# Feed-forward weights rounded by GpSimd, attention's last bias loaded as a column, all orders written anew

## Chip, cores and metric

One core of one Trainium2 chip runs the kernel. The metric is the device time of one execution in microseconds (us). The engines are TensorE (PE; its weight loads are listed apart as PEld), VectorE (DVE), ScalarE (ACT), GpSimd (POOL) and SyncE (SP).

## What is computed

The input is x, 16 sequences of 256 tokens with 128 features. Two blocks follow each other, each as x + layernorm(block(layernorm(x))).

```
n  = ln(x, g, b)
W1 = gelu(n @ h1_w1 + h1_b1) @ h1_w2 + h1_b2        # 128 -> 512 -> 128
W2 = gelu(n @ h2_w1 + h2_b1) @ h2_w2 + h2_b2
t  = tril(W1 @ W2^T) @ n
t  = ln(gelu(t), g, b);  x1 = x + t
out = x + gelu(ln(x1, g, b) @ fm_w1 + fm_b1) @ fm_w2 + fm_b2      # attention block

h = silu(x @ w1 * s1) * (x @ w2 * s2)               # feed-forward block, 128 -> 512
h = gelu(h @ h1 * hs1);  h = gelu(h @ h2 * hs2)     # 512 -> 512, twice
out = h @ w3 * s3                                   # 512 -> 128
```

## The kernel before

**Tiling.** The 4096 tokens are cut into 8 chunks of 512 (N = 512, four tiles of 128 tokens). Activations inside the blocks lie transposed, features on partitions and 512 tokens along the free axis. The last chunk's feed-forward part is cut into two halves of 256 tokens, numbered 7 and 8.

**Precision.** Each product is made of values split into a rounded high half and a low half, both fp32r. An output tile takes three matmuls per block of weights: low weights by high input, high by high, high by low. The feed-forward weights are ternary, so their low halves are expected to be zero. The kernel tests that: `lo_block` (L339) subtracts on GpSimd, `lo_sum` (L472) adds up the absolute values on ScalarE, `lo_test`, `lo_count` and `lo_raise` (L738 to L743) make a flag, and TensorE reads it and branches into `stream` (L1191) with or without the third matmul. With zero low halves the feed-forward products take two.

**Weights.** SyncE loads six pieces of the attention weights into `raw`, with parts of x between them, then six pieces of the feed-forward weights into the same buffer (five of 1024 columns, one of 512; `F_PIECES`, L117). `attn_w_hi` (L457) rounds an attention piece on ScalarE and `attn_w_lo` (L717) subtracts on VectorE. `ffn_w_hi` (L467) rounds a feed-forward piece on ScalarE, with one copy. A feed-forward piece 0 to 2 is loaded when two attention pieces are used up, pieces 3 to 5 when `lo_sum` of pieces 0 to 2 is done.

**Engines.** ScalarE does gelu and every eviction of a high half twice over: `up_hi` (L504) writes the rounded gelu, `up_act` (L512) writes the whole gelu back to the PSUM bank, and VectorE's `up_lo` subtracts the one from the other (all such subtractions run through `low`, L715). The feed-forward layers do the same with `layer_hi`, `layer_act` and `layer_lo`. VectorE also has the statistics and the layernorms; of these `n_first` (L761) and `n_second` (L772) read two SBUF operands, as `attn_w_lo` does. GpSimd has small layernorm steps (`x_s_` L326, `rstd` L345), `n_low` (L335), two steps on x (`xr_scale`, `xr_b`), and the x output.

**Bias of the last layer.** `fm_b2` is the attention's last bias as a column, read by `fm_evict` (L542). SyncE loads it as a row of 512 bytes into a corner of `M`. `fm_bias_product` (L1083) on TensorE turns it into a column with one matmul against a one, next to the four matmuls that make `fm_bias`, and `fm_bias_add` (L726) copies it out of the bank on VectorE.

**Order.** Nothing is scheduled at run time. Each engine has one list of calls, written out by hand or by a planner, that interleaves the chunks; semaphores (`Steps`) hold the engines together. `TURNS` (L43) gives for each of the eight PSUM banks the order in which groups of results use it, and `bank_free` (L1036) waits for the group before. So an engine that waits holds up everything behind it in its list.

```
            def ffn_w_hi(i):                                  # ScalarE, L467
                c0, c1, at = F_PIECES[i]
                act.wait_ge(ffn_in[i], 16)
                nc.scalar.activation(Fw[0][:, c0:c1], raw[:, at:at + c1 - c0], ACT.Copy).then_inc(*ffn_hi.done(0, i))
            def lo_block(n):                                  # GpSimd, L339
                i, c0, at = F_BLOCKS[n]
                pool.wait_ge(*ffn_hi.at(0, i))
                nc.gpsimd.tensor_tensor(Fw[1][:, c0:c0 + DI], raw[:, at:at + DI], Fw[0][:, c0:c0 + DI].bitcast(f32),
                                        ALU.subtract).then_inc(*ffn_lo.done(0, n))
```

## Time and profile before

| what | value |
|---|---|
| median of 3 runs | 365.7 us (365.67 to 366.59) |
| span of the profiled execution, first to last instruction | 362.6 us |
| mean granted TensorE clock | 0.996 |
| busy: PE / DVE / ACT / POOL | 97% / 88% / 84% / 41% of the span |
| instructions: PE / DVE / ACT / POOL | 1788 / 954 / 552 / 213 |
| HBM traffic | 6.57 MB read, 2.10 MB written, 24 GB/s over the span |

The times listed are those of the three runs; the profiled execution has its span alone in the page, 3.1 us under the median. What lies around the span (start and end of the program) is not in it. Busy time counts an engine as busy from the start to the end of an instruction. Matmuls are pipelined and their ends are modelled, so that a busy TensorE need not be one at its peak; the same holds to a lesser degree for the other engines, whose instructions start before the end of the one ahead. In a timeline or a list of waits, "<-" and a name behind an idle time say what ended it. The rows leave out the numbers of a buffer, so fm_b2 stands there as fm_b.

### The profile page before, as it was taken

To read this page: it belongs to the slowest core of one execution; us is meant where nothing else is said; L and a number is where in the kernel's file an instruction comes from. 1 tells how busy PE (TensorE), PEld (TensorE's weight loads), DVE (VectorE), ACT (ScalarE), POOL (GpSimd) and SP (SyncE) were. 2 spreads that over 40 slices of the span, in tenths; PEclk is the share of its full clock that TensorE was granted. 3 is DMA by queue.
4 is the path that set the end of the run, shared out by engine and by line. 5 is a ranking of instruction groups with operands and counts; after the bars stand their busy time and mean duration, and the time that the engine had idled before them with its cause. 6 is when DMAs were issued, how large, how long until landed. Compare 5 with 4: busy or idle time off the path is not lost.

```text
span 362.6 us, 6039 instructions
## 1 busy us (share of the span) xinstructions
PE 350.1 (97%) x1788; PEld 289.2 (80%) x1788; DVE 319.9 (88%) x954; ACT 305.2 (84%) x552; POOL 147.2 (41%) x213
## 2 busy tenths in 40 slices
PE   6989999999999999999999999999999999999993
PEld 5867687778888888888888888888888887788992
DVE  5889999999999999889989989998969998886936
ACT  5999999997779979988599888897799569959892
POOL 4168842860546052504750286003920174044411
PEclk9999999999999999999999999999999999999998
DMA  7507020000000000000010001000000001001111
GB/s 233 174 14 245 4 60 1 1 2 1 3 0 0 2 0 2 17 13 2 1 29 3 0 0 33 0 1 2 1 0 2 0 2 31 0 2 29 32 30 33
DMA packets 8804, 9.08 MB, mean 25 GB/s; under 512 B 577, under 2 KB 6722, under 8 KB 8770
## 3 DMA queue, kind: packets, MB, share of 16 engines
q1 hardware_dynamic: 8226, 8.41, 7.7%
q8 instruction: 16, 0.26, 0.3%
q10 hardware_dynamic: 544, 0.26, 0.2%
q14 instruction: 18, 0.15, 0.1%
HBM read 6.57 MB, written 2.10 MB: 24 GB/s over the span
## 4 chain that ended last, share of the span: by engine, by line
PE 67%; ACT 13%; DVE 10%; issue 5%; DMA 2%; POOL 1%; SPq 1%; POOLq 0%; DVEq 0%; ACTq 0%
PE bank L1224 8%; PE bank L1226 8%; PE bank L1240 6%; PE bank L1241 6%; PE bank L1123 4%; PE bank L1104 4%; PE bank L1108 4%; PE bank L1105 4%; PE bank L1120 4%; PE bank L1121 4%; PE bank L1206 4%; PE bank L1209 4%; ACT h_hidden_hi L510 3%; PE bank L1046 2%; ACT bank L515 2%
## 5 line engine op out<-in xcount | busy, mean ns | idle before, releaser
L715 DVE TENSOR_TENSOR ffn_gate_lo<-bank,ffn_gate_hi 128x512 fp32r<-128x512 f32 (+1 forms) x72 | 44.1, 626 | 6.0 <-ACT bank L584 4.9
L510 ACT ACTIVATE h_hidden_hi<-bank,cols 128x512 fp32r<-128x512 f32 x64 | 46.1, 760 | 3.5 <-PE bank L1108 3.2
L515 ACT ACTIVATE bank<-bank,cols 128x512 f32<-128x512 f32 x64 | 45.1, 739 | 0.3
L715 DVE TENSOR_TENSOR h_hidden_lo<-bank,h_hidden_hi 128x512 fp32r<-128x512 f32 x64 | 43.0, 681 | 2.5 <-ACT bank L515 2.5
L584 ACT ACTIVATE bank<-bank,cols 128x512 f32<-128x512 f32 (+1 forms) x72 | 43.7, 620 | 0.7
L1224 PE MATMUL bank<-ffn_gate_hi,ffn_w_hi 128*128 128x512 f32 (+1 forms) x108 | 40.5, 381 | 0.2 <-DVE ffn_gate_lo L715 0.2
L1226 PE MATMUL bank<-ffn_gate_lo,ffn_w_hi 128*128 128x512 f32 (+1 forms) x108 | 39.3, 370 | 0.2 <-DVE ffn_gate_lo L715 0.2
L578 ACT ACTIVATE ffn_h_hi<-bank,cols 128x512 fp32r<-128x512 f32 (+1 forms) x36 | 23.0, 646 | 13.5 <-PE bank L1226 8.3
L578 ACT ACTIVATE ffn_gate_hi<-bank,cols 128x512 fp32r<-128x512 f32 (+1 forms) x36 | 23.2, 647 | 10.6 <-PE bank L1226 8.3
L364 POOL TENSOR_TENSOR XR<-X,ln_x_r 128x512 f32<-128x512 f32 x8 | 8.3, 1042 | 53.6 <-DVE bank L861 53.4
L715 DVE TENSOR_TENSOR ffn_h_lo<-bank,ffn_h_hi 128x512 fp32r<-128x512 f32 (+1 forms) x36 | 22.0, 626 | 8.0 <-ACT bank L584 7.8
L1206 PE MATMUL bank<-yT_hi,ffn_w_hi 128*128 128x512 f32 (+1 forms) x72 | 26.9, 378 | 0.0
L1123 PE MATMUL bank<-h_hidden_lo,attn_w_hi 128*128 128x512 f32 x64 | 25.8, 402 | 1.1 <-DVE h_hidden_lo L715 1.0
L569 ACT ACTIVATE ffn_gate_hi<-bank 128x512 fp32r<-128x512 f32 (+1 forms) x36 | 19.8, 560 | 8.0 <-DVE bank L906 8.0
L1240 PE MATMUL bank<-ffn_h_hi,ffn_w_hi 128*128 128x512 f32 (+1 forms) x72 | 26.4, 375 | 0.0
L1104 PE MATMUL bank<-aT_hi,attn_w_lo 128*128 128x512 f32 x64 | 25.9, 405 | 0.5 <-DVE attn_w_lo L715 0.5
L1209 PE MATMUL bank<-yT_lo,ffn_w_hi 128*128 128x512 f32 (+1 forms) x72 | 26.2, 369 | 0.0
L1120 PE MATMUL bank<-h_hidden_hi,attn_w_lo 128*128 128x512 f32 x64 | 26.0, 406 | 0.0
L1224 PE MATMUL bank<-ffn_h_hi,ffn_w_hi 128*128 128x512 f32 (+1 forms) x72 | 26.0, 368 | 0.0
L1226 PE MATMUL bank<-ffn_h_lo,ffn_w_hi 128*128 128x512 f32 (+1 forms) x72 | 25.9, 367 | 0.0
L1241 PE MATMUL bank<-ffn_h_lo,ffn_w_hi 128*128 128x512 f32 (+1 forms) x72 | 25.8, 367 | 0.0
L1240 PE MATMUL bank<-ffn_gate_hi,ffn_w_hi 128*128 128x512 f32 (+1 forms) x72 | 25.8, 366 | 0.0
(164 smaller groups left out, 1132.3 us busy)
## 6 DMA issues: line engine op xcount, KB each, us to landing
raw<-ffn_w SPq DMA_DIRECT2D x5, 512.0 KB, 3.9
out<-X SPq DMA_DIRECT2D x7, 256.0 KB, 2.3
raw<-attn_w SPq DMA_DIRECT2D x6, 256.0 KB, 4.9
X<-x SPq DMA_DIRECT2D x3, 256.0 KB, 5.6
raw<-ffn_w SPq DMA_DIRECT2D x1, 256.0 KB, 3.2
X<-x ACTq DMA_DIRECT2D x1, 128.0 KB, 2.5
X<-x SPq DMA_DIRECT2D x1, 128.0 KB, 2.3
out<-X SPq DMA_DIRECT2D x1, 128.0 KB, 1.8
```

What stands on the lines that cost most here:

```text
L510: nc.scalar.activation(dst, bank(f"{L}u{j}", c)[:, :], ACT.Gelu, bias=bias_of(L, j)).then_inc(*hi[L].done(c, j))
L515: nc.scalar.activation(u[:, :], u[:, :], ACT.Gelu, bias=bias_of(L, j)).then_inc(*act2[L].done(c, j))
L578: nc.scalar.activation(dst, bank(f"{L}{j}", c)[:, span(c)], ACT.Gelu, scale=cols[:, C_HS[L] + j:C_HS[L] + j + 1]).then_inc(*hi[L].done(c, j))
L584: nc.scalar.activation(u, u, ACT.Gelu, scale=cols[:, C_HS[L] + j:C_HS[L] + j + 1]).then_inc(*act2[L].done(c, j))
L715: return nc.vector.tensor_tensor(dst, whole, high.bitcast(f32), ALU.subtract)
L1120: nc.tensor.matmul(bank(g, c)[:, :], Aw[1][:, w], buf[0][:, slot, :], start=(k == 0), stop=False)
L1206: nc.tensor.matmul(dst, Fw[0][:, w], yT[0][:, span(c)], start=not lo_pass, stop=False)
L1209: nc.tensor.matmul(dst, Fw[0][:, w], yT[1][:, span(c)], start=False, stop=True)\
L1224: nc.tensor.matmul(dst, Fw[0][:, w], high, start=(k == 0 and not lo_pass), stop=False)
L1226: last = nc.tensor.matmul(dst, Fw[0][:, w], low_, start=False, stop=(k == J - 1))
L1240: nc.tensor.matmul(dst, Fw[0][:, w], src[0][:, k, span(c)], start=(k == 0 and not lo_pass), stop=False)
L1241: last = nc.tensor.matmul(dst, Fw[0][:, w], src[1][:, k, span(c)], start=False, stop=(k == J - 1))
```

## The change

Six instructions move from ScalarE to GpSimd: `ffn_w_hi` becomes a `tensor_copy` on GpSimd, in that engine's list, and ScalarE's copies go. The bias row's load on SyncE, its matmul on TensorE and its copy on VectorE go; ScalarE's queue issues a load of `fm_b2` as a column of 128 times four bytes right at the start, and `fm_evict(0)` waits for it. All five lists and the eight strings of `TURNS` are written anew. Except for what is named above, each engine's list holds the same calls as before in another order. Of the lists and of `TURNS` the diff below keeps the first lines and those at which the order matters for the prediction.

```diff
--- before.py
+++ after.py
@@ -41,29 +41,28 @@
-    "rb.0 fb.0 h1d.1 h1u3.2 fmd.0 h2u0.3 h2u2.3 flag.0 fmd.1 q3.0 a2.0 b0.0 mT.2 fmu2.2 p3.1 fT.0 h1u1.5 fmu2.3 q1.2 "
-    "h1d.5 p0.3 s1.5 t.5 p0.4 p1.4 fmu1.5 s1.6 a1.4 b0.4 b3.4 p1.5 p3.5 a2.5 b3.5 fmu2.7 a0.6 yT.7 b3.6 q1.8 a2.7 "
-    "a3.8 b2.8",
...
+    "rb.0 h1u0.0 h1d.0 h1u1.1 h2u3.1 h2u1.2 fmu2.0 nT.3 oT.0 h2u3.3 q0.0 h1u0.4 a2.0 h1u3.4 yT.1 w3.0 fmu3.2 h2d.4 "
+    "b2.1 b3.1 q2.2 q3.2 a2.2 b3.2 p2.3 t.5 yT.4 w3.3 q1.4 s1.6 t.6 fmu2.6 fmu0.7 fmd.7 oT.7 b0.6 q0.8 a0.8 b1.7 b2.8 "
+    "fT.7",
...
@@ -136,7 +135,6 @@
         NF, XR, XRB = sb("NF", [P, T, D]), sb("XR", [P, T, D]), sb("XRB", [P, T, D])
         n_tok = halves("n_tok", [P, T, D])
         M, TG = sb("M", [P, T, D]), sb("TG", [P, N])
-        b2_row = M[0:1, 0, :]
         OTA = sb("OTA", [P, N])
         aT, mT, yT = halves("aT", [P, N]), halves("mT", [P, N]), halves("yT", [P, N])
         WT = {L: halves(f"{L}T", [P, N]) for L in ("h1", "h2")}
@@ -286,7 +284,6 @@
             attn_piece(0)
             attn_piece(1)
             attn_piece(2)
-            sp.dma_start(b2_row, rows[2:3, :]).then_inc(b2_in, 16)
             x_piece(1, 1, 2)
             for i in (3, 4, 5):
                 attn_piece(i)
@@ -336,6 +333,11 @@
                 pool.wait_ge(*n_hi.at(c))
                 nc.gpsimd.tensor_tensor(n_tok[1][:, :, :], NF[:, :, :], n_tok[0][:, :, :].bitcast(f32), ALU.subtract).then_inc(*n_lo.done(c))
 
+            def ffn_w_hi(i):
+                c0, c1, at = F_PIECES[i]
+                pool.wait_ge(ffn_in[i], 16)
+                nc.gpsimd.tensor_copy(Fw[0][:, c0:c1], raw[:, at:at + c1 - c0]).then_inc(*ffn_hi.done(0, i))
+
             def lo_block(n):
                 i, c0, at = F_BLOCKS[n]
                 pool.wait_ge(*ffn_hi.at(0, i))
@@ -429,24 +431,26 @@
-            x_s_(0); n_low(0); x_s_(1); x_s_(2); lo_block(0); lo_block(1); x_r(0); xr_scale(0); lo_block(2); xr_b(0)
-            lo_block(3); n_low(1); t_r(0); x_r(1); lo_block(4); lo_block(5); x1_r(0); lo_block(6); lo_block(7); x_s_(3)
-            lo_block(8); n_low(2); t_r(1); xr_scale(1); xr_b(1); lo_block(9); o_r(0); x_r(2); x1_r(1); lo_block(10); y_r(0)
-            y_centre(0); y_scale(0); o_shift_(0); n_low(3); x_s_(4); xr_scale(2); xr_b(2); o_r(1); t_r(2); x_r(3); x1_r(2)
...
+            x_s_(0); n_low(0); x_r(0); x_s_(1); ffn_w_hi(0); lo_block(0); ffn_w_hi(1); lo_block(1); lo_block(2); x_s_(2)
+            lo_block(3); ffn_w_hi(2); lo_block(4); n_low(1); xr_scale(0); t_r(0); lo_block(5); xr_b(0); ffn_w_hi(3)
+            x1_r(0); lo_block(6); ffn_w_hi(4); lo_block(7); x_r(1); ffn_w_hi(5); n_low(2); x_s_(3); lo_block(8)
+            lo_block(9); t_r(1); xr_scale(1); xr_b(1); x_r(2); o_r(0); x1_r(1); lo_block(10); o_shift_(0); y_centre(0)
+            y_r(0); y_scale(0); n_low(3); x_s_(4); xr_scale(2); o_r(1); xr_b(2); o_shift_(1); t_r(2); x1_r(2); y_centre(1)
...
             act.dma_start(X[:, 2:4, :], xv[:, 2:4, :]).then_inc(x_in_half, 16)
+            act.dma_start(fm_b2[:, :], rows[2:3, :].rearrange("o d -> d o")).then_inc(b2_in, 16)
             act.wait_ge(*consts.at(0, 0))
             nc.scalar.activation(warm[:, :], ones[:, :], ACT.Gelu)
...
-            def ffn_w_hi(i):
-                c0, c1, at = F_PIECES[i]
-                act.wait_ge(ffn_in[i], 16)
-                nc.scalar.activation(Fw[0][:, c0:c1], raw[:, at:at + c1 - c0], ACT.Copy).then_inc(*ffn_hi.done(0, i))
 
@@ -542,6 +541,8 @@
             def fm_evict(c):
                 if c:
                     act.wait_ge(*oT.at(c - 1))
+                else:
+                    act.wait_ge(b2_in, 16)
                 act.wait_ge(*down["fm"].at(c, J - 1))
                 nc.scalar.activation(OTA[:, :], bank("fmd", c)[:, :], ACT.Identity, bias=fm_b2[:, :]).then_inc(*fm_out.done(c))
 
...
-            rows_out(); attn_w_hi(0); attn_w_hi(1); n_high(0); nT_high(0); attn_w_hi(2); attn_w_hi(3); attn_w_hi(4)
-            up_hi("h1", 0, 0); up_hi("h1", 1, 0); up_act("h1", 0, 0); up_act("h1", 1, 0); up_hi("h1", 2, 0); up_hi("h2", 0, 0)
-            up_hi("h1", 3, 0); up_act("h1", 2, 0); up_act("h2", 0, 0); up_act("h1", 3, 0); up_hi("h2", 1, 0); up_hi("h2", 2, 0)
-            up_act("h2", 1, 0); up_hi("h2", 3, 0); nT_high(1); up_act("h2", 2, 0); up_act("h2", 3, 0); ffn_w_hi(0)
-            attn_w_hi(5); down_hi("h1", 0); down_hi("h2", 0); up_hi("h1", 0, 1); up_hi("h2", 0, 1); ffn_w_hi(1)
-            up_act("h2", 0, 1); score_hi(0, 0); up_hi("h1", 1, 1); score_hi(1, 0); up_hi("h1", 2, 1); up_act("h1", 0, 1)
...
-            layer_act("b", 2, 8); layer_hi("b", 3, 8); w3_evict(7); layer_act("b", 3, 8); w3_evict(8); last_store()
+            rows_out(); attn_w_hi(0); attn_w_hi(1); attn_w_hi(2); nT_high(0); attn_w_hi(3); n_high(0); up_hi("h1", 0, 0)
+            up_act("h1", 0, 0); up_hi("h1", 1, 0); up_hi("h1", 2, 0); up_act("h1", 1, 0); up_hi("h1", 3, 0)
+            up_hi("h2", 0, 0); up_act("h1", 2, 0); up_act("h2", 0, 0); up_hi("h2", 1, 0); up_act("h1", 3, 0)
+            up_hi("h2", 2, 0); up_act("h2", 1, 0); up_act("h2", 2, 0); nT_high(1); up_hi("h2", 3, 0); attn_w_hi(4)
+            up_act("h2", 3, 0); down_hi("h1", 0); attn_w_hi(5); up_hi("h1", 0, 1); down_hi("h2", 0); up_hi("h2", 0, 1)
+            up_act("h1", 0, 1); up_act("h2", 0, 1); up_hi("h1", 1, 1); score_hi(0, 0); up_act("h1", 1, 1); score_hi(1, 0)
...
+            layer_act("b", 3, 8); w3_evict(7); w3_evict(8); last_store()
@@ -725,7 +729,6 @@
 
             def fm_bias_add():
                 dve.wait_ge(*fm_b.at(0))
-                nc.vector.tensor_scalar(fm_b2[:, :], bank("fb", 0)[:, J:J + 1], 1.0, None, ALU.mult)
                 nc.vector.tensor_tensor(fm_bias[:, :], bank("fb", 0)[:, 0:J], cols[:, C_B1["fm"]:C_B1["fm"] + J], ALU.add).then_inc(*fm_b_added.done(0))
 
             def gate_constants():
...
-            x_st(0); x_ag(0); n_first(0); n_second(0); attn_w_lo(0); attn_w_lo(1); nT_low(0); x_st(1); x_ag(1); n_first(1)
-            attn_w_lo(2); attn_w_lo(3); up_lo("h1", 0, 0); up_lo("h1", 1, 0); n_second(1); up_lo("h1", 2, 0); up_lo("h2", 0, 0)
-            x_st(2); up_lo("h1", 3, 0); x_ag(2); up_lo("h2", 1, 0); nT_low(1); up_lo("h2", 2, 0); up_lo("h2", 3, 0)
-            attn_w_lo(4); down_lo("h1", 0); down_lo("h2", 0); attn_w_lo(5); fm_bias_add(); score_mask(0, 0); score_mask(1, 0)
...
-            layer_lo("b", 1, 8); layer_lo("b", 2, 8); layer_lo("b", 3, 8); last_stats(0); last_aggregate(0); last_centre(0)
-            last_stats(1); last_aggregate(1); last_centre(1); last_sum(0); last_sum(1)
+            x_st(0); x_ag(0); n_first(0); n_second(0); attn_w_lo(0); nT_low(0); x_st(1); attn_w_lo(1); attn_w_lo(2)
+            attn_w_lo(3); up_lo("h1", 0, 0); x_ag(1); n_first(1); fm_bias_add(); up_lo("h1", 1, 0); x_st(2)
+            up_lo("h1", 2, 0); n_second(1); up_lo("h2", 0, 0); up_lo("h1", 3, 0); up_lo("h2", 1, 0); x_ag(2); nT_low(1)
+            up_lo("h2", 2, 0); x_st(3); up_lo("h2", 3, 0); down_lo("h1", 0); attn_w_lo(4); down_lo("h2", 0); attn_w_lo(5)
...
+            m_norm(2); t_ag(3); x_ag(5); up_lo("h1", 3, 4); layer_lo("b", 0, 0); layer_lo("b", 1, 0); mT_low(2)
...
+            layer_lo("b", 3, 8); last_stats(0); last_aggregate(0); last_stats(1); last_centre(0); last_aggregate(1)
+            last_centre(1); last_sum(0); last_sum(1)
@@ -1086,9 +1093,7 @@
                 pe.wait_ge(cols_in, 16)
                 for j in range(J):
                     w = ATTN["fmu"] + j * P
-                    nc.tensor.matmul(bank("fb", 0)[:, j:j + 1], raw[:, w:w + P], cols[:, C_B:C_B + 1], start=True, stop=True)
-                pe.wait_ge(b2_in, 16)
-                last = nc.tensor.matmul(bank("fb", 0)[:, J:J + 1], b2_row, ones[0:1, :], start=True, stop=True)
+                    last = nc.tensor.matmul(bank("fb", 0)[:, j:j + 1], raw[:, w:w + P], cols[:, C_B:C_B + 1], start=True, stop=True)
                 last.then_inc(*fm_b.done(0))
 
             def up_mm(L, j, c):
...
-            up_mm("h1", 1, 0); up_mm("h2", 0, 0); up_mm("h2", 1, 0); up_mm("h1", 2, 0); up_mm("h1", 3, 0); fm_bias_product()
-            down_mm("h1", 0, 0); up_mm("h2", 2, 0); down_mm("h1", 1, 0); up_mm("h2", 3, 0); down_mm("h1", 2, 0); n_transpose(1)
...
-            scores(1, 2); m_transpose(1); down_mm("h1", 3, 3); up_mm("h2", 3, 3); down_mm("h2", 1, 3); up_mm("fm", 0, 1)
-            up_mm("fm", 1, 1); lo_count(); t_product(2); y_transpose(0); down_mm("h2", 2, 3); up_mm("fm", 2, 1)
+            up_mm("h1", 1, 0); up_mm("h1", 2, 0); up_mm("h1", 3, 0); up_mm("h2", 0, 0); fm_bias_product()
+            down_mm("h1", 0, 0); up_mm("h2", 1, 0); up_mm("h2", 2, 0); down_mm("h1", 1, 0); down_mm("h1", 2, 0)
...
+            down_mm("h2", 0, 3); down_mm("h2", 1, 3); up_mm("fm", 0, 1); up_mm("fm", 1, 1); t_product(2); lo_count()
+            up_mm("fm", 2, 1); y_transpose(0); down_mm("h2", 2, 3); down_mm("h2", 3, 3)
...
```

Up to `yT_low(0)`, the VectorE step behind the first feed-forward input, the new VectorE list holds the same calls as the old one but for `x_ag(5)`, which comes later now. Up to `yT_high(0)` the new ScalarE list holds the same calls but for the six copies. Up to `y_transpose(0)` the new TensorE list holds one call more, `up_mm("fm", 2, 1)`. Behind `y_transpose(7)` TensorE's remaining calls, and behind `yT_high(7)` ScalarE's, are the same as before, in another order.

## Rows read from the trace of the kernel before

**Rows 1.** The page, busy us of each engine (share of the span) x instructions
```profile
PE 350.1 (97%) x1788; PEld 289.2 (80%) x1788; DVE 319.9 (88%) x954; ACT 305.2 (84%) x552; POOL 147.2 (41%) x213
```

**Rows 2.** The page, chain of work that ended last, by engine
```profile
PE 67%; ACT 13%; DVE 10%; issue 5%; DMA 2%; POOL 1%; SPq 1%; POOLq 0%; DVEq 0%; ACTq 0%
```

**Rows 3.** By stretch: length; busy PE, PEld, DVE, ACT, POOL (x count); clock; DMA share, GB/s
```profile
10.00:30.00 20.00, 18.75 (x98) 15.10 (x97) 17.45 (x45) 19.98 (x35) 10.07 (x11) 1.00 0.36 115
30.00:80.00 50.00, 48.48 (x243) 37.84 (x242) 48.30 (x166) 49.74 (x88) 30.13 (x36) 1.00 0.13 39
80.00:300.00 220.00, 220.00 (x1089) 182.76 (x1088) 202.56 (x594) 181.73 (x317) 83.72 (x123) 1.00 0.02 5
300.00:350.00 50.00, 49.11 (x282) 41.70 (x281) 38.39 (x104) 42.79 (x91) 17.44 (x28) 1.00 0.06 18
```
**Rows 4.** Chain in order of time: start us, us on the chain, what
```profile
20.98 0.98 ACT ffn_w_hi L470
24.78 0.95 ACT ffn_w_hi L470
37.37 0.52 ACT ffn_w_hi L470
40.75 0.97 ACT ffn_w_hi L470
```

**Rows 5.** All waits of ScalarE, 10 to 80 us: total, times, longest
```profile
ACT attn_w_hi L465 <- DMA raw<-attn_w: 1.0, 1, 1.0
```

**Rows 6.** Longest wait of VectorE, 10 to 80 us: total, times, longest
```profile
DVE sc_lo L715 <- ACT sc_hi L528: 0.8, 2, 0.4
```

**Rows 7.** Timeline, first 12 us: start us, us, engine, line, operation
```profile
3.19 0.33 SPq L289 DMA_DIRECT2D M<-rows  x1
...
7.23 0.63 ACT L483 ACTIVATE n_tok_hi<-NF 128x512 fp32r<-128x512 f32 x1 [0.61 <-DVE NF L776]
...
9.88 0.63 ACT L465 ACTIVATE attn_w_hi<-raw 128x512 fp32r<-128x512 f32 x1 [1.02 <-DMA raw<-attn_w]
...
11.17 1.25 ACT L510 ACTIVATE h_hidden_hi<-bank,cols 128x512 fp32r<-128x512 f32 x2
```

**Rows 8.** Timeline of GpSimd: a fill, an operation with a broadcast operand, and one with two operands
```profile
1.02 0.32 POOL L318 MEMSET mask<- 128x256 f32 x1
...
26.69 1.04 POOL L364 TENSOR_TENSOR XR<-X,ln_x_r 128x512 f32<-128x512 f32 x1
27.69 1.29 POOL L342 TENSOR_TENSOR ffn_w_lo<-raw,ffn_w_hi 128x512 fp32r<-128x512 f32 x1
```

**Rows 9.** Timeline of VectorE, operations with two SBUF operands
```profile
11.73 1.29 DVE L715 TENSOR_TENSOR attn_w_lo<-raw,attn_w_hi 128x512 fp32r<-128x512 f32 x2
...
24.41 0.94 DVE L715 TENSOR_TENSOR attn_w_lo<-raw,attn_w_hi 128x512 fp32r<-128x512 f32 x1
...
32.83 1.14 DVE L769 SCALAR_TENSOR_TENSOR NF<-X,ln_x_mv,bc 128x128 f32<-128x128 f32 x4 [0.22 <-issue]
```

**Rows 10.** Timeline of GpSimd, what ran beside them
```profile
22.03 2.77 POOL L342 TENSOR_TENSOR ffn_w_lo<-raw,ffn_w_hi 128x512 fp32r<-128x512 f32 x2 [1.82 <-ACT ffn_w_hi L470]
...
31.44 1.30 POOL L337 TENSOR_TENSOR n_tok_lo<-NF,n_tok_hi 128x512 fp32r<-128x512 f32 x1
```

**Rows 11.** Timeline of VectorE, two small steps
```profile
25.27 0.14 DVE L728 TENSOR_SCALAR fm_b<-bank 128x1 f32<-128x1 f32 x1
25.34 0.14 DVE L729 TENSOR_TENSOR fm_bias<-bank,cols 128x4 f32<-128x4 f32 x1
...
79.05 0.36 DVE L705 BATCH_NORM_AGGREGATE ln_x_mv<-ln_x_st 128x2 f32<-128x6 f32 x4
```

**Rows 12.** Timeline of GpSimd, two of its long waits
```profile
52.62 1.30 POOL L337 TENSOR_TENSOR n_tok_lo<-NF,n_tok_hi 128x512 fp32r<-128x512 f32 x1 [2.95 <-ACT n_tok_hi L483]
...
61.94 1.04 POOL L364 TENSOR_TENSOR XR<-X,ln_x_r 128x512 f32<-128x512 f32 x1 [3.43 <-DVE bank L861]
```

**Rows 13.** Readers of the bias column: duration min/median/max ns, first and last start us
```profile
L546 ACT ACTIVATE OTA<-bank,fm_b x8: 680/688/722, 59.4 to 315.1; 128x512 f32<-128x512 f32 x8
```

**Rows 14.** Timeline, last 8 us
```profile
354.82 0.48 ACT L590 ACTIVATE raw<-bank,cols 128x256 f32<-128x256 f32 x1
355.20 0.44 ACT L584 ACTIVATE bank<-bank,cols 128x256 f32<-128x256 f32 x1
...
356.89 0.60 DVE L939 TENSOR_SCALAR raw<-bank,ln_f_mv 128x128 f32<-128x128 f32 x2
```

More of the change, by code:

```diff
@@ L445, in _ @@
+            x_end(6); x_shift(); last_rstd(0); last_rstd(1)
         @block.scalar
@@ new lines, in _ @@
+            layer_hi("b", 2, 2); layer_act("b", 2, 2); layer_hi("b", 3, 2); gate_tanh(0, 3); gate_tanh(1, 3)
+            up_hi("fm", 0, 4); layer_act("b", 3, 2); up_hi("fm", 1, 4); up_act("fm", 0, 4); up_act("fm", 1, 4)
+            up_hi("fm", 2, 4); score_hi(0, 5); w3_evict(2); up_act("fm", 2, 4); gate_tanh(2, 3); gate_hi(0, 3)
+            up_hi("h1", 0, 6); gate_hi(1, 3); up_hi("fm", 3, 4); up_act("fm", 3, 4); gate_tanh(3, 3); fm_evict(4)
+            score_hi(1, 5); gate_hi(2, 3); up_hi("h1", 1, 6); up_act("h1", 0, 6); gate_hi(3, 3); t_act(5)
@@ new lines, in _ @@
+            layer_act("b", 2, 3); down_hi("h1", 6); mT_high(5); yT_high(4); up_hi("h2", 3, 6); layer_hi("b", 3, 3)
+            layer_act("b", 3, 3); up_act("h2", 3, 6); gate_tanh(0, 4); up_hi("fm", 0, 5); up_act("fm", 0, 5)
+            up_hi("fm", 1, 5); gate_tanh(1, 4); up_hi("fm", 2, 5); up_act("fm", 1, 5); w3_evict(3); gate_hi(0, 4)
+            gate_tanh(2, 4); nT_high(7); down_hi("h2", 6); gate_hi(1, 4); up_act("fm", 2, 5); up_hi("fm", 3, 5)
+            up_act("fm", 3, 5); up_hi("h1", 0, 7); gate_hi(2, 4); gate_tanh(3, 4); up_act("h1", 0, 7); fm_evict(5)
@@ new lines, in _ @@
+            layer_act("b", 1, 5); yT_high(6); layer_hi("b", 2, 5); layer_act("b", 2, 5); layer_hi("b", 3, 5); mT_high(7)
+            gate_tanh(0, 6); gate_tanh(1, 6); layer_act("b", 3, 5); up_hi("fm", 0, 7); up_hi("fm", 1, 7)
+            up_act("fm", 0, 7); up_act("fm", 1, 7); gate_tanh(2, 6); up_hi("fm", 2, 7); gate_hi(0, 6); up_act("fm", 2, 7)
+            gate_hi(1, 6); up_hi("fm", 3, 7); up_act("fm", 3, 7); gate_tanh(3, 6); gate_hi(2, 6); fm_evict(7)
+            gate_hi(3, 6); w3_evict(5); layer_hi("a", 0, 6); layer_act("a", 0, 6); layer_hi("a", 1, 6)
```

512 lines of the change are left out of this document (255 added, 257 removed), and 39 rows, old and new, of the table TURNS.

## Prediction

> **What bounds the kernel now.** I read the busy table first. TensorE is busy for 350.1 of 362.6 us [rows 1], and 67% of the chain that ended last is TensorE's [rows 2]. That leaves 12.5 us of open idle time, but busy time flatters an engine whose matmuls overlap, so the next view is the stretches [rows 3]. From 80 to 300 us TensorE shows no idle time at all and its weight loads are busy for 182.76 of 220 us, 0.831 per us. From 10 to 80 us they are busy for 15.10 + 37.84 = 52.94 us, 0.756 per us. At the later pace those loads would have taken 52.94 / 0.831 = 63.7 us, so about 6.3 us of that stretch is TensorE running thin, of which only 70 − 18.75 − 48.48 = 2.8 us is shown as idle. From 300 to 350 us the loads keep 0.834, and 0.9 us is idle.
>
> Who holds it back before 80 us? ScalarE is busy for 19.98 of 20 and 49.74 of 50 us [rows 3], and its only wait there is one of 1.0 us for a load [rows 5]. VectorE is busy for 17.45 of 20 and 48.30 of 50 us: 2.55 us idle up to 30 us, 1.70 us after. GpSimd has 10 of 20 and 20 of 50 us free. The chain in order of time runs over ScalarE's copies of the feed-forward weights [rows 4]. So before 80 us ScalarE is the bound, VectorE stands 4.25 us behind it, and behind 80 us only TensorE counts. A time saved before 80 us is kept only if TensorE reaches its full stretch earlier; nothing saved on ScalarE after that is worth anything. The granted clock is 1.00 in all four stretches, the 2.4 GHz level, and is no term.
>
> **ScalarE's six copies.** On the chain a copy of 1024 columns takes 0.98, 0.95 and 0.97 us, that of 512 columns 0.52 [rows 4]. Five long and one short make 5 x 0.97 + 0.52 = 5.4 us taken from an engine without idle time: two copies (1.9 us) before 30 us, four (3.4 us) between 30 and 80. VectorE is next: with the same calls up to yT_low(0) it can win no more than its idle time. Before 30 us the bound is 1.9 us (ScalarE) against 2.55 (VectorE's idle), and I take 1.5. After 30 us it is 3.4 against 1.70, and I take half of the 1.70, 0.85: the idle time is made of short waits for a result just ordered (the longest kind 0.8 us in two waits, [rows 6]), and part of such a wait stays when ScalarE is faster. Sum −2.35 us, between 0 and −3.6.
>
> **VectorE's removed and moved steps.** The copy of the bias column goes: the next step starts 25.34 − 25.27 = 0.07 us later [rows 11]. x_ag(5), 0.36 us [rows 11], moves behind yT_low(0), into a stretch where VectorE has 17 us free of 220. Together −0.4 us. TensorE's small matmul goes too, under 0.1 us, in a stretch in which it waits anyway: nothing. up_mm("fm", 2, 1) ahead of y_transpose(0) fills a wait if there is one; it is part of the 2.35.
>
> **GpSimd's six copies.** No row shows a copy on GpSimd. From below, a fill of 256 columns takes 0.32 us [rows 8], so 1024 take at most four times that, 1.3 us. From above, an operation with two operands takes 1.29 us per 512 columns, 2.6 us per 1024; that with one broadcast operand 1.04, or 2.1. I take 1.3, the fill being the nearest in operands moved, and keep 2.6. (The Trainium skill, "GPSIMD Engine Reference", section "Elementwise — side-by-side cycle accounting", has 1.03 cycles per element at 1.2 GHz for simple bodies, by estimate 0.88 us per 1024 columns; the sum would be the same.) The six make 5.5 x 1.3 = 7.1 us (up to 14.2) on an engine with 30 us free before 80. Does its list become late? It waits 2.95 us for ScalarE's n_high(2) and 3.43 us for the attention output [rows 12]; from the second on, the new list has one lo_block less than the old before x1_r(1). So up to the dearer price the copies end before these two waits do, and the chain lo_block(10), lo_sum(5), flag is not late. x_s_(1) moves behind n_low(0), whose n_high(0) ScalarE now runs later, and n_second(1), which needs it, is moved behind two more steps on VectorE. No term, up to +1 us.
>
> **The shared reads of VectorE and GpSimd.** attn_w_lo takes 1.29 us for two, but 0.94 us for the one that starts while GpSimd subtracts two SBUF operands, 0.25 us more than the 0.69 of a single one; n_first(2) starts at 32.83, 0.09 us behind the end of n_low(1) at 32.74, after an unexplained 0.22 us [rows 9, 10]. So a VectorE instruction with two SBUF operands stands still while GpSimd reads. Between 12 and 57 us there are ten such groups (attn_w_lo of four pieces, n_first and n_second of three chunks). The copies fill 7.1 of these 45 us, 16%, so 1.6 meetings at 0.25 us: +0.4 us. The Trainium skill says the same under "SBUF — State Buffer", section "Who interferes with whom": a VectorE instruction with two SBUF inputs and a GpSimd instruction that reads SBUF exclude each other for the whole instruction. By that rule each meeting would cost the rest of a copy, half of 1.3 us on average: +1.0 us for the 1.6 meetings, and a sum of −1.65 us. The 0.09 us behind n_low(1) speaks for it, the 0.25 us against its full price; with the dearer copies it is a rival below.
>
> **The loads.** On SyncE the row's issue, 0.33 us [rows 7], goes ahead of x_piece(1) and attention pieces 3 to 5, so piece 3, for which ScalarE waits 1.02 us, is issued 0.33 us earlier. Against that, n_high(0), 0.63 us [rows 7], ran before that wait and now runs after it, ahead of up_hi("h1", 0, 0), while attn_w_hi(4) leaves that place. The first up_hi stays near 11.17 us. Term 0, from −0.5 to +0.5. The column load is 128 pieces of four bytes on ScalarE's queue; its first reader starts at 59.4 us [rows 13], and 50 us of cover hide whatever it takes. If that cover were gone the whole landing would stand before fm_evict(0).
>
> **The stretches behind 80 us.** With TensorE full the new lists can only lose there, or win from the 0.9 us idle between 300 and 350. Nothing in the rows says which; term 0, from −0.9 to +1. In the last 8 us, layer_act("b", 3, 8) goes ahead of w3_evict(7) and starts 0.38 us earlier (355.20 − 354.82), while last_centre(0), about 0.5 us, goes behind last_stats(1) and so onto the chain [rows 14]: +0.1 us, from −0.4 to +0.5.
>
> **Sum.** −2.35 − 0.4 + 0.4 + 0.1 = −2.25 us against a span of 362.6. All lower ends together make −5.8 us, all upper ends +3.0 (0 − 0.4 + 0.4 + 1 + 0.5 + 1 + 0.5), without the dearer price of (c). The profiled span is 3.1 us under the median of the runs, which I take as unchanged, so the sum applies to 365.7 as it is: 363.4 us. A difference of 0.3%, 1.1 us, is about what a measurement of this kernel can tell from none.
>
> **Rivals.**
> (a) VectorE holds as before, chance 0.25. ScalarE was only level with it, and VectorE's idle time is latency that stays. Then only the 0.4 us is left, less the shared reads: 365.3 us, no measurable change. For it: VectorE idles 1.70 of 50 us after 30 us. Against it: ScalarE has no idle time at all, VectorE has some.
> (b) All of VectorE's idle time is recovered, chance 0.15: 4.25 + 0.4 = 4.65 us, 361.0 us. For it: all lists are new, and TensorE has 6.3 us to win. Against it: it needs every wait of VectorE gone.
> (c) The copies block VectorE, chance 0.12, slower. Place: n_first, n_second and attn_w_lo up to 57 us, on the engine that is next to the bound. At 2.6 us a copy they fill 14.2 of 45 us, 32%, which makes 3.2 meetings; if each costs half a copy, 1.3 us, that is 4.1 us against the 2.75 won: with +0.1 for the end, +1.5 us, 367.2 us. It decides from 3.8 us of blocked VectorE time on. For it: the 0.22 us wait up to the end of n_low(1). Against it: at most 0.25 us was lost where the 0.94 us subtraction met GpSimd. The Trainium skill's rule named above is this rival's rule.
> (d) The forecast, chance 0.48, with 361.9 to 364.6 us of its own.
>
> **Range and chances.** Over all cases 360.9 to 366.2 us: it takes in (b) and (a) with a lost 0.5 us, and leaves out most of (c). Faster by over 0.3%: (d) and (b), 0.63. Within 0.3%: (a), 0.25. Slower: (c), 0.12.
>
> **What would show it.** Right: ScalarE shows idle time between 10 and 80 us of at least 2 us; weight loads per us rise from 0.756 towards 0.78 in that stretch; the stretch in which TensorE shows no idle time begins some 2 us before 80 us; VectorE's idle time there falls below 4.25 us; GpSimd's copies of 1024 columns take 1.0 to 1.5 us. Wrong: copies near 2.6 us with VectorE waits at L769, L776 or L715 that end with them; TensorE idle time between 80 and 300 us, which would be the new lists' own loss; or a gain that arises behind 300 us.

## The result, and the profile after

The kernel after takes 376.64 us (median of 4 runs, 376.09 to 376.75) against 365.79 us of the kernel before beside it (365.67 to 366.59): 10.85 us slower, ratio 1.029, 95% interval 1.0276 to 1.0305. The forecast was 363.4 us and the range ended at 366.2; the result lies outside it, on the other side of no change.

Page of the kernel after: busy us of each engine, then the chain that ended last by engine.
```profile
PE 355.8 (95%) x1786; PEld 293.3 (78%) x1786; DVE 329.8 (88%) x953; ACT 303.1 (81%) x546; POOL 153.1 (41%) x219
...
PE 75%; DVE 14%; issue 4%; POOL 2%; DMA 2%; ACT 1%; POOLq 0%; DVEq 0%; ACTq 0%
```
Beside [rows 1]: VectorE is busy for 9.9 us more, though its list has one instruction fewer. Its instructions became longer, not more numerous. In the chain ScalarE's 13% [rows 2] are down to 1%.

The first three stretches of [rows 3], and two short ones behind them (columns as there).
```profile
10.00:30.00 20.00, 16.71 (x71) 12.51 (x70) 18.35 (x41) 14.84 (x26) 12.74 (x13) 0.91 0.23 68
30.00:80.00 50.00, 45.09 (x212) 34.87 (x212) 46.41 (x137) 41.21 (x74) 29.93 (x34) 0.93 0.19 58
80.00:300.00 220.00, 219.13 (x1090) 181.91 (x1089) 202.42 (x572) 185.50 (x322) 82.42 (x121) 1.00 0.02 6
20.00:24.00 4.00, 3.06 (x9) 2.29 (x9) 3.60 (x9) 1.07 (x3) 1.60 (x3) 0.59 0.00 0
41.00:48.00 7.00, 5.82 (x14) 4.27 (x15) 6.97 (x21) 2.30 (x4) 1.93 (x3) 0.51 0.17 68
```
The loss is made before 80 us: 27 + 31 = 58 matmuls fewer were begun there than before (71 against 98, 212 against 243). Behind 80 us both kernels keep nearly the same pace (1089 and 1090 matmuls between 80 and 300). ScalarE is busy for only 56.05 of 70 us, although six copies were taken from it: these explain 5.4 us, the other 8 are waiting. And the granted clock, 1.00 in all of [rows 3], is near half in two short stretches (0.59 and 0.51). Who is waited for stands in the first line of TensorE's waits, 10 to 80 us (total, times, longest); the next in the list has 0.6 us:
```profile
PE bank L1060 <- DVE NF L779: 6.8, 8, 1.5
```
L1060 is n_transpose, L779 is n_second (L776 before). So all but a little of TensorE's shown waiting is for the second normalisation step. Timeline of VectorE, its steps with two SBUF operands; below, n_second(1) means the step for the second chunk of 512 tokens, or part 1:
```profile
9.72 2.98 DVE L719 TENSOR_TENSOR attn_w_lo<-raw,attn_w_hi 128x512 fp32r<-128x512 f32 x3
...
16.81 4.27 DVE L779 SCALAR_TENSOR_TENSOR NF<-NF,ln_x_s,bc 128x128 f32<-128x128 f32 x4
...
37.21 1.85 DVE L772 SCALAR_TENSOR_TENSOR NF<-X,ln_x_mv,bc 128x128 f32<-128x128 f32 x4 [0.74 <-issue]
...
39.58 3.49 DVE L779 SCALAR_TENSOR_TENSOR NF<-NF,ln_x_s,bc 128x128 f32<-128x128 f32 x4
...
64.00 2.83 DVE L779 SCALAR_TENSOR_TENSOR NF<-NF,ln_x_s,bc 128x128 f32<-128x128 f32 x4
...
193.56 2.51 DVE L772 SCALAR_TENSOR_TENSOR NF<-X,ln_x_mv,bc 128x128 f32<-128x128 f32 x4
```
Timeline of GpSimd beside the second of these, and beside the third and fourth:
```profile
14.93 1.04 POOL L339 CAST ffn_w_hi<-raw 128x1024 fp32r<-128x1024 f32 x1
16.05 1.30 POOL L344 TENSOR_TENSOR ffn_w_lo<-raw,ffn_w_hi 128x512 fp32r<-128x512 f32 x1
17.29 1.11 POOL L339 CAST ffn_w_hi<-raw 128x1024 fp32r<-128x1024 f32 x1
18.36 2.57 POOL L344 TENSOR_TENSOR ffn_w_lo<-raw,ffn_w_hi 128x512 fp32r<-128x512 f32 x2
...
37.06 1.05 POOL L366 TENSOR_TENSOR XR<-X,ln_x_r 128x512 f32<-128x512 f32 x1
...
39.66 1.38 POOL L344 TENSOR_TENSOR ffn_w_lo<-raw,ffn_w_hi 128x512 fp32r<-128x512 f32 x1
```
The same step in the kernel before:
```profile
14.20 1.13 DVE L776 SCALAR_TENSOR_TENSOR NF<-NF,ln_x_s,bc 128x128 f32<-128x128 f32 x4
```
Here it starts later and is 4.27 us for the same four instructions, and GpSimd works beside it with hardly a gap from 14.93 to 20.93. Timeline of TensorE beside it:
```profile
17.64 0.30 PE L1060 MATMUL bank<-ident,NF 128*128 128x128 f32 x1 [0.20 <-DVE NF L779]
18.59 0.33 PE L1060 MATMUL bank<-ident,NF 128*128 128x128 f32 x1 [0.65 <-DVE NF L779]
19.86 0.33 PE L1060 MATMUL bank<-ident,NF 128*128 128x128 f32 x1 [0.94 <-DVE NF L779]
21.13 0.48 PE L1060 MATMUL bank<-ident,NF 128*128 128x128 f32 x1 [0.94 <-DVE NF L779]
...
21.84 0.63 PE L1110 MATMUL bank<-aT_hi,attn_w_hi 128*128 128x512 f32 x1
```
The transposes come 0.95, 1.27 and 1.27 us apart: each time about one GpSimd instruction (1.11, and 2.57 for two). So not one meeting per group, but one for each of its four instructions. Behind the fourth the clock has fallen, and matmuls of 512 columns follow each other at 0.42 to 0.43 us (21.84 to 22.26, the next in the trace) instead of 0.23. It happens again before part 2, where the matmuls keep 0.43 us until 48 us.

Three explanations stood at this point. **Theory 1:** GpSimd's denser row of instructions shuts out VectorE's steps on two SBUF operands, and the clock adds to it. **Theory 2:** the new orders of all engines are worse by themselves. **Theory 3:** the bias column, or the loads that come later with it.

### The profile page after: what moved, and what is told of

It reads as the page before. It is cut to its first block, busy times and chain, and to the rows that moved or that the text cites. A ratio compares the mean times of both kernels' runs of the same rounds, so it can differ in the third digit from the quotient of the medians.

```text
span 374.3 us, 6035 instructions
## 1 busy us (share of the span) xinstructions
PE 355.8 (95%) x1786; PEld 293.3 (78%) x1786; DVE 329.8 (88%) x953; ACT 303.1 (81%) x546; POOL 153.1 (41%) x219
## 4 chain that ended last, share of the span: by engine, by line
PE 75%; DVE 14%; issue 4%; POOL 2%; DMA 2%; ACT 1%; POOLq 0%; DVEq 0%; ACTq 0%
PE bank L1233 9%; PE bank L1231 9%; PE bank L1247 7%; PE bank L1248 7%; PE bank L1125 4%; PE bank L1128 4%; PE bank L1126 4%; PE bank L1213 4%; PE bank L1216 4%; PE bank L1109 4%; PE bank L1113 4%; PE bank L1110 4%; DVE NF L779 3%; PE bank L1053 2%; PE bank L1151 2%
## 5 line engine op out<-in xcount | busy, mean ns | idle before, releaser
L509 ACT ACTIVATE h_hidden_hi<-bank,cols 128x512 fp32r<-128x512 f32 x64 | 43.6, 701 | 5.4 <-PE bank L1113 4.6
L585 ACT ACTIVATE bank<-bank,cols 128x512 f32<-128x512 f32 (+1 forms) x72 | 44.6, 632 | 1.0
L514 ACT ACTIVATE bank<-bank,cols 128x512 f32<-128x512 f32 x64 | 42.5, 673 | 0.4
L1231 PE MATMUL bank<-ffn_gate_hi,ffn_w_hi 128*128 128x512 f32 (+1 forms) x108 | 40.0, 376 | 0.0
L349 POOL TENSOR_SCALAR ln_o_ve<-ln_o_mv 128x4 f32<-128x4 f32 x8 | 1.8, 228 | 69.5 <-DVE ln_o_mv L709 69.5
L1109 PE MATMUL bank<-aT_hi,attn_w_lo 128*128 128x512 f32 x64 | 26.9, 421 | 0.9 <-DVE h_hidden_lo L719 0.6
L1125 PE MATMUL bank<-h_hidden_hi,attn_w_lo 128*128 128x512 f32 x64 | 27.0, 422 | 0.2 <-DVE h_hidden_lo L719 0.2
L1126 PE MATMUL bank<-h_hidden_hi,attn_w_hi 128*128 128x512 f32 x64 | 25.9, 405 | 0.0
```

The costliest lines, as they stand in the source:

```text
L509: nc.scalar.activation(dst, bank(f"{L}u{j}", c)[:, :], ACT.Gelu, bias=bias_of(L, j)).then_inc(*hi[L].done(c, j))
L514: nc.scalar.activation(u[:, :], u[:, :], ACT.Gelu, bias=bias_of(L, j)).then_inc(*act2[L].done(c, j))
L585: nc.scalar.activation(u, u, ACT.Gelu, scale=cols[:, C_HS[L] + j:C_HS[L] + j + 1]).then_inc(*act2[L].done(c, j))
L1109: nc.tensor.matmul(bank(g, c)[:, :], Aw[1][:, w], xT[0][:, :], start=True, stop=False)
L1125: nc.tensor.matmul(bank(g, c)[:, :], Aw[1][:, w], buf[0][:, slot, :], start=(k == 0), stop=False)
L1231: nc.tensor.matmul(dst, Fw[0][:, w], high, start=(k == 0 and not lo_pass), stop=False)
```

## The parts of the change, each alone

**The move alone, in the old orders.**
```diff
-ffn_w_hi(0) ... ffn_w_hi(5)            # ScalarE's list
-x_s_(0); n_low(0); x_s_(1); x_s_(2); lo_block(0); lo_block(1); ...       # GpSimd's list
+x_s_(0); n_low(0); x_s_(1); x_s_(2); ffn_w_hi(0); lo_block(0); lo_block(1); ...
```


> The kernel before with one part of the change alone: the six rounded copies of the feed-forward weights go from ScalarE to GpSimd, each just ahead of its first low half; all other orders as before. Theory 1 (GpSimd instructions standing back to back hold up VectorE's steps that read two SBUF operands, one GpSimd instruction per step, and TensorE's granted clock falls in the wait): n_second(1) of about 1.1 us becomes 2 us or more where it lies beside the copies and low halves, and the whole is 368 to 374 us. Theory 2 (the new orders cost the time, not the move): 363 to 367 us, with the normalisation steps as long as before. Theory 3 (the bias column or the later loads cost it): 363 to 367 us too.

Measured: 365.57 us, ratio 1.0004, interval 0.998 to 1.0027. No difference. Windows of this kernel:
```profile
10.00:30.00 20.00, 19.35 (x100) 15.43 (x98) 18.28 (x46) 18.52 (x33) 12.41 (x13) 1.00 0.40 128
30.00:80.00 50.00, 47.73 (x240) 37.52 (x240) 47.45 (x165) 46.76 (x83) 33.82 (x40) 1.00 0.12 34
```
ScalarE now has 70 − 65.28 = 4.7 us without work, where it had 0.3 in [rows 3]. VectorE is busy for 65.73 us (65.75 before), and TensorE's weight loads for 52.95 (52.94 before). Most of what was taken from ScalarE, 4.4 of 5.4 us, turned into ScalarE's idle time. That is what rival (a) said. And the copies shut out hardly anything, because of where they stand: timeline of its GpSimd, and of VectorE.
```profile
18.24 0.19 POOL L331 TENSOR_SCALAR ln_x_vs<-ln_x_mv 128x4 f32<-128x4 f32 x1 [6.59 <-DVE ln_x_mv L705]
...
19.48 1.04 POOL L342 CAST ffn_w_hi<-raw 128x1024 fp32r<-128x1024 f32 x1
20.61 2.99 POOL L347 TENSOR_TENSOR ffn_w_lo<-raw,ffn_w_hi 128x512 fp32r<-128x512 f32 x2
```
```profile
13.86 1.13 DVE L776 SCALAR_TENSOR_TENSOR NF<-NF,ln_x_s,bc 128x128 f32<-128x128 f32 x4
...
21.00 1.44 DVE L721 SCALAR_TENSOR_TENSOR attn_w_lo<-raw,cols,attn_w_hi 128x512 fp32r<-128x512 f32 x1
```
The old list has x_s_(2) ahead of the first low half. It waits 6.59 us for x_ag(2), which VectorE runs behind n_second(1); by its code it also waits for n_second(1) itself. By this wait the row of GpSimd work cannot begin before n_second(1) is through. Only attn_w_lo(4) meets it and takes 1.44 instead of 0.74 us.

**The bias column alone.**
```diff
-sp.dma_start(b2_row, rows[2:3, :]).then_inc(b2_in, 16)
+act.dma_start(fm_b2[:, :], rows[2:3, :].rearrange("o d -> d o")).then_inc(b2_in, 16)
```


> The kernel before with the last layer's bias loaded as a column by ScalarE's queue, its matmul and VectorE's copy gone; orders as before. Theories 1 and 2: 365 to 367 us, nothing that can be measured. Theory 3 (a column of 128 transfers of 4 bytes delays the loads around it): over 368 us, with the first weights or tokens landing over 1 us later.

364.96 us, ratio 0.9993, interval 0.9972 to 1.0015: nothing, and Theory 3 falls for the bias.

**Both parts, old orders.** The two diffs above together.

> The kernel before with both parts of the change (copies on GpSimd, bias loaded as a column) and all old orders. If relief of ScalarE reaches the end at all: 362.5 to 364.5 us. If ScalarE's idle time is only handed to VectorE and TensorE waits as before: 364.5 to 366 us, no difference that can be told from the kernel before.

365.98 us, ratio 1.001, interval 0.9995 to 1.0025. The second case of the expectation. So in the old lists the functional change is worth nothing in either direction, and the 10.85 us come with the new lists.

**The new orders with the copies back on ScalarE.**
```diff
-ffn_w_hi(0) ... ffn_w_hi(5)            # GpSimd's list
+ffn_w_hi(0) ... ffn_w_hi(5)            # ScalarE's list, at places like the old ones
```


> The kernel after with the six copies back on ScalarE, at places like those of the kernel before; the new orders, bank turns and bias column stay. Theory 1: GpSimd has room between its instructions again, n_second(1) falls from 4.27 us to under 2.5 us, n_second(2) from 3.49 to under 2.5 us, the stretch at half clock after 41 us shrinks, and the time is 366 to 371 us. Theory 2 (orders): 374 to 379 us, as slow as the kernel after. Theory 3: the same.

375.8 us, ratio 1.0294, interval 1.0249 to 1.0338: Theory 1 missed by 5 us in the form in which I had put it, with the copies as the culprits, and the time is the one that Theory 2 gave. Timelines of GpSimd and of VectorE in this kernel:
```profile
34.88 1.28 POOL L339 TENSOR_TENSOR ffn_w_lo<-raw,ffn_w_hi 128x512 fp32r<-128x512 f32 x1 [4.46 <-ACT ffn_w_hi L469]
36.12 1.26 POOL L334 TENSOR_TENSOR n_tok_lo<-NF,n_tok_hi 128x512 fp32r<-128x512 f32 x1
```
```profile
17.07 1.14 DVE L779 SCALAR_TENSOR_TENSOR NF<-NF,ln_x_s,bc 128x128 f32<-128x128 f32 x4
...
37.47 1.85 DVE L772 SCALAR_TENSOR_TENSOR NF<-X,ln_x_mv,bc 128x128 f32<-128x128 f32 x4 [3.69 <-issue]
39.84 3.14 DVE L779 SCALAR_TENSOR_TENSOR NF<-NF,ln_x_s,bc 128x128 f32<-128x128 f32 x4
```
n_second(1) is healed (1.14 us), as expected. But n_low(1) stands behind lo_block(4), which waits 4.46 us for ScalarE's copy of the third piece of the weights. Its ScalarE half, n_high(1), ended at 32.24; n_low(1) starts at 36.12. n_first(2) waits for it, since NF is one buffer. The "issue" of 3.69 us is this dependency: the step begins 0.09 us after n_low(1) ends (36.12 + 1.26 = 37.38). The same 0.09 us stands in the kernel before, between 32.74 and 32.83 [rows 9, 10]. So a second mechanism joined the first: a result of the critical path queued behind work on the weights. It is not quite the one of the kernel after. The load of this piece was issued at 26.31 and takes some 3.5 us (the median of these loads in this kernel), so it had landed near 30 us; what came late is ScalarE's copy, at 33.75, behind n_high(1) and lo_sum(0) in ScalarE's list, where this experiment had put it. In the kernel after GpSimd's own copy runs right behind the landing (33.45), n_high(1) ends at 34.92, and n_low(1), at 35.81, is late by 0.9 us only.

## Whose order it is

**GpSimd's list alone, both ways.** Only its head, up to about 50 us, is exchanged; each kernel has the copies on GpSimd.
```diff
-x_s_(0); n_low(0); x_r(0); x_s_(1); ffn_w_hi(0); lo_block(0); ffn_w_hi(1); lo_block(1); lo_block(2); x_s_(2)
-lo_block(3); ffn_w_hi(2); lo_block(4); n_low(1); xr_scale(0); t_r(0); lo_block(5); xr_b(0); ffn_w_hi(3)
+x_s_(0); n_low(0); x_s_(1); x_s_(2); ffn_w_hi(0); lo_block(0); lo_block(1); x_r(0); xr_scale(0); ffn_w_hi(1); lo_block(2); xr_b(0)
+lo_block(3); n_low(1); t_r(0); x_r(1); ffn_w_hi(2); lo_block(4); lo_block(5); x1_r(0); ffn_w_hi(3)
```
(shown as made to the kernel after; the other kernel has it the other way round, in the old orders of the rest.)

> The kernel after with the head of GpSimd's order alone (up to the second part of x, about 50 us) put back to the order of the kernel before, the copies still on GpSimd, each ahead of its first low half. In it the low half n_low(1) no longer stands behind the copy and the low half of the third piece of the weights. New theory, 2a (the loss is made by GpSimd's new order: n_low(1) behind a load, and with it n_first(2), n_second(2) and the transposes of part 2, on which TensorE stands idle and loses its clock): 366 to 370 us, the stretch 40 to 50 us at full clock. Theory 2b (the orders of VectorE, ScalarE and TensorE lose it, whatever GpSimd does): 373 to 378 us. Theory 1 (sharing with the copies): above 372 us with n_second(1) still over 2 us.

Measured: 369.58 us, ratio 1.0108, interval 1.0068 to 1.0147. 7.1 us of the loss are gone. Its VectorE:
```profile
17.12 1.13 DVE L778 SCALAR_TENSOR_TENSOR NF<-NF,ln_x_s,bc 128x128 f32<-128x128 f32 x4
...
36.57 1.13 DVE L778 SCALAR_TENSOR_TENSOR NF<-NF,ln_x_s,bc 128x128 f32<-128x128 f32 x4
```
The time lies in Theory 2a's range, but n_low(1) is not what healed: it starts 2.5 us behind the end of its ScalarE half here (33.55 and 31.02) and 0.9 us behind it in the kernel after. What is gone is the sharing. Both normalisation steps are back to 1.13 us with all copies on GpSimd, since the old head has x_s_(2) ahead of the first copy.

> The kernel before with the copies on GpSimd and the head of GpSimd's order of the kernel after; VectorE, ScalarE and TensorE in their old orders. Theory 2a: 370 to 377 us, n_low(1) after the landing of the third piece and TensorE idle before the transposes of part 2. Theory 2b: 364 to 368 us. Theory 1 alone: 364 to 368 us, since the copies alone did nothing.

Measured: 368.35 us, ratio 1.0065, interval 1.0038 to 1.0091. Its VectorE:
```profile
14.61 2.72 DVE L777 SCALAR_TENSOR_TENSOR NF<-NF,ln_x_s,bc 128x128 f32<-128x128 f32 x4
22.48 1.62 DVE L722 SCALAR_TENSOR_TENSOR attn_w_lo<-raw,cols,attn_w_hi 128x512 fp32r<-128x512 f32 x1
...
33.51 1.85 DVE L770 SCALAR_TENSOR_TENSOR NF<-X,ln_x_mv,bc 128x128 f32<-128x128 f32 x4 [0.16 <-issue]
...
57.41 2.61 DVE L777 SCALAR_TENSOR_TENSOR NF<-NF,ln_x_s,bc 128x128 f32<-128x128 f32 x4
```
This time is below Theory 2a's range and above the other two. Against 1.13, 0.74 and 1.14 us in the kernel before, VectorE lost 1.59 + 0.88 + 0.71 = 3.2 us in the first three, and 1.5 more in n_second(3); the kernel lost 2.6 us beside its own before, 2.8 us beside the move in the old list. The granted clock stays at 1.00 here. GpSimd's list is to blame for most of it. With the old lists of the others it costs under 3 us, with their new lists 7 us. The rows show part of the reason: in the new lists n_second(1) loses 3.14 us instead of 1.59 and n_second(2) 2.39 instead of nothing, and the clock falls.

**n_low(1) one place earlier.** Made to the new orders with the copies on ScalarE:
```diff
-lo_block(3); lo_block(4); n_low(1); xr_scale(0)
+lo_block(3); n_low(1); lo_block(4); xr_scale(0)
```


> The kernel after with the six copies on ScalarE (375.8 us) and one more edit: on GpSimd n_low(1) goes ahead of the low half that waits for the third piece of the weights. Theory 2a: n_low(1) starts near 32.2 us, when its ScalarE half is done, instead of 36.1; TensorE's wait of 4.4 us before the transposes of part 2 goes, its clock stays up between 36 and 48 us, and the time is 366 to 370 us. Theory 2b: 373 to 377 us.

369.41 us against 375.8: one step moved by one place gives 6.4 us back. That is most of the 10.2 us which that kernel stands above the one before. Not all of it is the queue: n_first(2) and n_second(2) also meet less of GpSimd there (1.14 and 1.92 us instead of 1.85 and 3.14), and the granted clock from 41 to 48 us is 1.00 instead of 0.50. And it says little of the kernel after, where n_low(1) was late by 0.9 us only.

## Is it really the reading of SBUF?

**The same work, with waits.** In the kernel after GpSimd waits at four places for VectorE's step:
```diff
+def hold(line, c, j=0):
+    pool.wait_ge(*line.at(c, j))
-x_s_(0); n_low(0); x_r(0); x_s_(1); ffn_w_hi(0); ...; n_low(1); xr_scale(0); t_r(0); lo_block(5)
+x_s_(0); hold(attn_lo, 0, 3); n_low(0); x_r(0); x_s_(1); hold(n_v_ready, 1, T - 1); ffn_w_hi(0); ...; n_low(1)
+hold(n_v, 2); xr_scale(0); t_r(0); hold(n_v_ready, 2, T - 1); lo_block(5)
```


> The kernel after, in which GpSimd waits at four places until VectorE is through with a step on two SBUF operands (the fourth low half of the attention weights, the normalisation steps of parts 1 and 2) before it starts its own next instruction. No work is left out or moved. Theory 1: n_second(1) and n_second(2) are 1.1 to 1.4 us instead of 4.27 and 3.49, the two stretches at half clock go, 366 to 371 us. Theory 2a: the first stretch heals, the second only if n_low(1) is not late: 372 to 376 us. Theory 2b: 374 to 378 us.

368.16 us, ratio 1.0072, interval 1.0052 to 1.0092. 8.5 us back, by nothing but waits on the engine that has time. Its VectorE:
```profile
10.55 1.88 DVE L722 TENSOR_TENSOR attn_w_lo<-raw,attn_w_hi 128x512 fp32r<-128x512 f32 x3
...
16.98 1.13 DVE L782 SCALAR_TENSOR_TENSOR NF<-NF,ln_x_s,bc 128x128 f32<-128x128 f32 x4
...
33.33 1.14 DVE L775 SCALAR_TENSOR_TENSOR NF<-X,ln_x_mv,bc 128x128 f32<-128x128 f32 x4 [0.77 <-issue]
34.99 1.54 DVE L782 SCALAR_TENSOR_TENSOR NF<-NF,ln_x_s,bc 128x128 f32<-128x128 f32 x4
...
56.57 2.83 DVE L782 SCALAR_TENSOR_TENSOR NF<-NF,ln_x_s,bc 128x128 f32<-128x128 f32 x4
```
The four groups of the kernel after up to 43 us, 2.98 + 4.27 + 1.85 + 3.49 = 12.6 us, take 5.7 us here. n_low(1) still stands behind the third piece, and VectorE still waits 0.77 us for it (0.74 in the kernel after), so Theory 2a is not what the waits take away; 2a and 2b had given 372 us and more. n_second(3) has no wait ahead of it and is as long as in the kernel after (2.83 us).

**GpSimd as dense, but reading nothing.**
```diff
-nc.gpsimd.tensor_copy(Fw[0][:, c0:c1], raw[:, at:at + c1 - c0])
+nc.gpsimd.memset(Fw[0][:, c0:c1].bitcast(f32), 0.0)
-nc.gpsimd.tensor_tensor(Fw[1][:, c0:c0 + DI], raw[:, at:at + DI], Fw[0][:, c0:c0 + DI].bitcast(f32), ALU.subtract)
+nc.gpsimd.memset(Fw[1][:, c0:c0 + DI].bitcast(f32), 0.0)
```


> The kernel after with GpSimd's six copies and eleven low halves of the feed-forward weights replaced by fills of the same results with zeros, which read nothing from SBUF. It leaves out the rounding and the low halves of these weights: both are zero. GpSimd's instructions stand as densely, the low halves are about half as long. If only GpSimd's reading holds VectorE up: n_second(1) under 1.6 us although fills lie beside it, 367 to 371 us. If any GpSimd instruction does: n_second(1) over 2.5 us, 371 to 375 us.

366.61 us, ratio 1.003, interval 1.0013 to 1.0046. Its GpSimd and its VectorE:
```profile
16.23 0.53 POOL L344 MEMSET ffn_w_lo<- 128x512 f32 x1
17.24 0.96 POOL L339 MEMSET ffn_w_hi<- 128x1024 f32 x1 [0.48 <-DMA raw<-ffn_w]
```
```profile
17.11 1.13 DVE L778 SCALAR_TENSOR_TENSOR NF<-NF,ln_x_s,bc 128x128 f32<-128x128 f32 x4
...
34.91 2.14 DVE L778 SCALAR_TENSOR_TENSOR NF<-NF,ln_x_s,bc 128x128 f32<-128x128 f32 x4
```
n_second(1) runs for 1.13 us with a fill beside it almost throughout (17.24 to 18.20). n_second(2) still takes 2.14: beside it runs XRB, which reads. So writing does not shut VectorE out, reading does. This is what the Trainium skill says in "SBUF — State Buffer", section "Who interferes with whom", and this case agrees with it: 4.27 us beside reads, 1.13 us beside writes. The time itself is no clean measure of the sharing, since the low halves are also shorter (0.53 us instead of 1.30). A form with two fills per low half, as long as the real ones, needed more SBUF than is left and has no time. The time is of use in another way: the new lists of VectorE, ScalarE and TensorE stand in this kernel, and it is only 0.9 us above its own before.

**Two moves instead of waits.**
```diff
-x_s_(1); ffn_w_hi(0); lo_block(0); ffn_w_hi(1); lo_block(1); lo_block(2); x_s_(2)
-lo_block(3); ffn_w_hi(2); lo_block(4); n_low(1); xr_scale(0)
+x_s_(1); x_s_(2); ffn_w_hi(0); lo_block(0); ffn_w_hi(1); lo_block(1); lo_block(2)
+lo_block(3); n_low(1); ffn_w_hi(2); lo_block(4); xr_scale(0)
```


> The kernel after with two steps moved in GpSimd's order and nothing else: x_s_(2), which waits for VectorE's x_ag(2) behind n_second(1), goes back ahead of the first copy, as in the kernel before; and n_low(1) goes ahead of the copy of the third piece. Theory 1 (sharing): the first copy starts after n_second(1) has ended, n_second(1) is under 1.6 us, and the time is 367 to 370 us, as with the waits put in by hand (368.2). If the place of x_s_(2) were of no account, n_second(1) would stay over 3 us and the time over 371 us.

372.69 us, ratio 1.0197, interval 1.0169 to 1.0225. The first half came as expected, the time did not. Its VectorE:
```profile
15.85 1.13 DVE L779 SCALAR_TENSOR_TENSOR NF<-NF,ln_x_s,bc 128x128 f32<-128x128 f32 x4
...
31.20 3.72 DVE L772 SCALAR_TENSOR_TENSOR NF<-X,ln_x_mv,bc 128x128 f32<-128x128 f32 x4
```
n_low(1), now early, released n_first(2) at 31.20, just where GpSimd goes on without a gap with the copy, the low half and XR. The step that took 1.14 us behind a wait takes 3.72 beside them. A place that frees a step on one engine can be the place that shuts it out.

## What the clock adds

**Work for TensorE in its waits.** Matmuls on the identity, written to the transposes' bank ahead of them, whose result nobody reads.
```diff
+FILLS = {1: (0, 2, 4, 4), 2: (5, 4, 4, 4)}        # the first kernel of this kind: nine before each
 for t in range(T):
+    for _ in range(FILLS.get(c, (0, 0, 0, 0))[t]):
+        nc.tensor.matmul(bank("nT", c)[:, t * P:(t + 1) * P], ident[:, :], ident[:, :], start=True, stop=True)
     pe.wait_ge(*n_v_ready.at(c, t))
```


> The kernel after with nine matmuls of 128 columns, whose result nobody reads, ahead of each of the four transposes of parts 1 and 2, so that TensorE has work while it would wait for VectorE's NF. VectorE's steps stay as long as in the kernel after. Theory of the clock (some 5 us of the loss come from the 10.2 us at the lower level, not from the wait itself): granted clock 1.0 from 20 to 24 and from 41 to 48 us, 370 to 373 us. Without it (the wait is all of the loss, or the fills only push work back): 375 to 379 us.

382.64 us, ratio 1.0461, interval 1.0432 to 1.0491. The clock stayed at 1.00, but nine fills take 2.17 us, more than any wait that they were to fill (at most 1.5), so this kernel settles nothing on the price of the clock. Hence the second, sized by it:

> The kernel after with matmuls that nobody reads only where TensorE waited: before the four transposes of part 1 none, 2, 4 and 4, before those of part 2 5, 4, 4 and 4 (0.24 us each in the run with nine, so 0.5 to 1.2 us per gap, about as long as the waits). VectorE's steps stay as long. In the kernel after the lower level lasts from 20.7 to 24.1 and from 41.2 to 48.0 us, 10.2 us, in which half the work is done: 5.1 us. Theory of the clock: granted clock 1.0 there, TensorE's transposes at the same times, 371 to 373 us. If the lower level costs nothing in the end (another engine is as late): 376 to 378 us.

374.03 us, ratio 1.0254, interval 1.0216 to 1.0293. Timeline of its TensorE, and two windows:
```profile
18.83 1.06 PE L1061 MATMUL bank<-ident 128*128 128x128 f32 x8
...
21.21 0.33 PE L1063 MATMUL bank<-ident,NF 128*128 128x128 f32 x1
```
```profile
20.00:24.00 4.00, 3.95 (x22) 3.22 (x23) 4.00 (x10) 1.73 (x4) 1.60 (x3) 1.00 0.00 0
41.00:48.00 7.00, 7.00 (x42) 6.09 (x41) 6.75 (x23) 4.64 (x8) 1.29 (x4) 1.00 0.05 18
```
Here the transposes of part 1 stand where they stood in the kernel after (21.21 against 21.13), VectorE's steps are as long (4.27 and 3.50 us), and only the clock differs. It gives 376.64 − 374.03 = 2.6 us, or somewhat more if the fills themselves cost anything. The expectation said 5.1 for all of the work not done at the lower level and 371 to 373 us; the time missed that by 1 us, and half of the 5.1 did not reach the end. Side by side, the runs divide the 10.85 us: 2.6 go when the clock stays up (374.03), 5.9 more when GpSimd waits for VectorE (368.16, also at a clock of 1.00 from 20 to 24 and from 41 to 48 us), and 2.4 stay. So the sharing is the cause, and a quarter of the loss is the clock, which falls in the waits that the sharing makes.

## Why the prediction was wrong

**The step that failed is "The shared reads of VectorE and GpSimd"**, the term +0.4. It measured 7.3 us of VectorE's time up to 43 us. Alone the four groups take 1.88, 1.13, 1.14 and 1.10 us, so they lost 1.10 + 3.14 + 0.71 + 2.39. Two groups further on, 2.83 and 2.51 us long instead of 1.14 and 1.13, lost 3.1 more; together 10.4, about the 9.9 us by which VectorE is busier. Three things in the term were wrong:
- *The count.* I counted a group as one instruction and spread the copies evenly over 45 us: 1.6 meetings. n_first and n_second are four instructions, and GpSimd gets in between each two of them. And the meetings aren't a matter of chance; the lists set them. In the new one the copies stand in one row with the low halves at the moment of n_second(1). The "No term, up to +1 us" for x_s_(1) and n_second(1) looked at the same place and weighed only the delay, and misread the list: x_s_(1) stood behind n_low(0) before too, and what is new between them is x_r(0).
- *The price.* The 0.25 us from [rows 9] was a meeting with a low half that had 0.39 us left to run. A whole GpSimd instruction costs 1.0 to 1.3 us.
- *The partners.* I counted the six copies alone. All of GpSimd's readers shut VectorE out, the low halves too, which the new list moves as well; with no copy on GpSimd at all n_second(2) still took 3.14 us.

The rule of the Trainium skill ("SBUF — State Buffer", section "Who interferes with whom") was before me and got +1.0 us. The trace agrees with it: each of n_second(1)'s four instructions waited for a GpSimd instruction to end (the transposes behind them start 0.19 to 0.29 us after GpSimd's ends at 17.35, 18.40 and 20.93). Rival (c), which is this mechanism, got 0.12. Its turning point (3.8 us of blocked VectorE time) held, and so did its place for four of the six groups. Its 4.1 us were 7.3 up to 57 us, and its way there was wrong: the copies aren't dear.

**The reading of 0.22 us** before n_first(2) [rows 9] as a sign of the sharing was wrong. It is the wait for n_low(1). It should have told me that VectorE waits for n_low(1), so that its place in GpSimd's list counts.

**"ScalarE's six copies", −2.35,** was 0, and so was the gain in all of (b): the move alone gives 365.57 us. ScalarE being busy for 69.7 of 70 us did not make it the bound. TensorE's weight loads didn't move at all when it was relieved. Two of the signs of being right came true all the same, ScalarE's idle time (14 us) and the price of the copies: they could not tell a gain from ScalarE waiting for others. The weight loads per us, (12.51 + 34.87) / 70 = 0.677, fell instead of rising, and VectorE's idle time rose to 5.2 us.

**"GpSimd's six copies".** The price was near: 1.04 us per 1024 columns against 1.3 taken (the estimate from the Trainium skill, "GPSIMD Engine Reference", section "Elementwise — side-by-side cycle accounting", was 0.88). The question whether the list becomes late was asked of the waits at 52 and 61 us [rows 12] and not of n_low(1) at 31 us [rows 10], where the answer was yes, though by 0.9 us only.

**The clock, "no term".** True of the kernel before; 2.6 us here. A forecast of longer waits on TensorE has to allow for it.

**The stretches behind 80 us,** term 0, and **the loads and the bias,** term 0, held within their bounds: TensorE is idle for 0.87 us between 80 and 300 us, where it had no idle time, and the bias column has no effect. VectorE's −0.4 for its small steps is less than these runs can tell.

The kernel with the four waits still stands 2.4 us above the kernel before. Part of this is still sharing: n_second(3) takes 2.83 us there, and TensorE waits 0.86 us for it (58.93 us); attn_w_lo(4) takes 1.34 instead of 0.74. With the shorter fills that read nothing only 0.9 us stay. How the rest divides between the other lists was not tried and stays open.

## What to carry to other kernels

Where GpSimd has time to spare, look not at how busy it is but at what stands beside its row: a VectorE step on two SBUF operands, split into small instructions, can pay a whole GpSimd instruction for each of them. A wait or a small step that depends on VectorE, put ahead of GpSimd's long readers, keeps them apart (8.5 us here); it may already be in the list by accident, as x_s_(2) was. But look where the released step lands: with two moves instead of four waits only 4 us came back. And before work is taken from a busy engine, look whether TensorE would start anything earlier: a full ScalarE was worth nothing here.

## What was not expected of the hardware

VectorE finished only one instruction of 0.34 us for each GpSimd reader of 1.0 to 1.3 us, four times in a row (transposes 0.95, 1.27 and 1.27 us apart), and GpSimd's readers were not longer for it (1.11 and 2.57 us for two, against 1.04 and 1.30), while a GpSimd fill beside it cost VectorE nothing. TensorE's granted clock went from the 2.4 to the 1.2 GHz level after waits of 0.20, 0.65, 0.94 and 0.94 us with only single transposes between them, and it stayed at 1.00 when these waits were filled.
